# Layer 0's experts: all tokens sorted into 39 blocks of 128 rows, one expert per block, outputs gathered back inside the cross-attention

## The chip, the cores and the metric

The kernel runs on one core of one Trainium2 chip. The metric is the device time of one execution in microseconds (us); three executions of the kernel before give a median of 1479.89 us.

## The reference, cut to what matters

A perceiver of two layers works on `x`, 128 batches of 32 tokens of 128 values, so 4096 tokens. Each layer adds three things to `x`: a cross-attention over a context of 257 rows for each batch, a self-attention, and a feed-forward part made of experts. The change is in the experts of layer 0 and touches the cross-attention of layer 1 that comes next. The experts of layer 0 are:

```python
capacity = ceil(T / E * 1.25)                 # T = 4096 tokens, E = 8 experts: 640
...
top1_idx = argmax(probs, axis=-1)             # the expert that each token wants
keep = position of the token in its expert (by falling probability) < capacity
final_e = where(keep, top1_idx, 0)            # dropped tokens go to expert 0
...
for e in range(E):
    h = relu(tokens @ W1[e] + b1[e])          # 128 -> 512
    y = h @ W2[e] + b2[e]                     # 512 -> 128
    out = out + where((final_e == e)[:, None], y, 0.0)
```

Experts 1 to 7 hold at most 640 tokens each; expert 0 holds its own and all dropped ones, so its size has no bound below 4096. The sum over experts is added to `x`, and the layer norm ahead of the next cross-attention reads the result.

## The kernel before

The 4096 tokens lie as 32 groups of 128 rows (`G = 32`), `X[:, g, :]` on the 128 partitions. All products are in fp32. The kernel is a row of phases, each a block with its own semaphores and a barrier of all engines at its end; inside a phase each engine runs a program written out by hand, and the engines meet only at semaphores. Matmuls run on TensorE (PE), and GpSimd (POOL) issues the DMAs whose rows are picked by a table of indices.

- `attend_layer0` does layer 0's two attentions. It leaves the normed tokens in `H_all`, their transposes in `HT_all`, and the router's logits. On the side its sync queue zeroes `rows_out` in memory.
- `route_layer0` (names that begin with `r_`) finds each expert's cut-off probability by 13 rounds of bisection: VectorE (DVE) counts, PE sums the counts over partitions (L987), DVE narrows. Then it computes for each token of experts 1 to 7 a slot number in a table of 7 x 640 rows. PE fills its gaps with `dense` pieces: expert 0 on every token of the first 20 groups, 512 tokens at a time (L948 up, L957 down).
- `experts_layer0` (`f_`) first turns the slot table round into `token_of`, the token of each slot, by 32 accumulating matmuls (L1193). It computes expert 0 on the other 12 groups (L1174, L1183) and adds expert 0's result to `X` under `MASK`. Then for each expert 1 to 7: five indirect gathers of rows of `rows_h` (L1330), transposes (L1211), the up product (L1221) in halves of 320 columns, ReLU on ScalarE (ACT), the down product (L1233), the bias on DVE (L1407), and five indirect scatters into `rows_out` (L1338). After the experts, `weights` computes 14 pieces of a weight product for the layer 1 self-attention (L1254, L1261). At the end the sync queue (SP) loads `rows_out` back into `HT_all` in 8 pieces (L1163).
- `cross_layer1` (`c_`) goes over 32 groups of 4 batches, four steps to a group. Its prologue loads `last`, the last context row of each batch (L1691), and norms group 0. The loaded expert outputs are added to `X` by eight wide additions, the first in the phase before (L1413), the others in group 0 (L2057).
- `experts_layer1` (also `f_`) works on sorted blocks: for each block of 256 rows a table gives the expert, an engine reads the number into a register, DVE copies that expert's first weights into a small ring `w1b` (L1573), and PE picks the second weights by the register (L1481 transpose, L1490 up, L1500 down).

## Time and profile before

| | |
|---|---|
| runs | 1474.99, 1479.89, 1480.83 us; median 1479.89 |
| profiled execution | 1482.46 us, of which the span of the trace is 1480.7 |
| PE | busy 1315.8 us, 89% of the span |
| PE weight loads | 1008.5 us, 68% |
| DVE | 1041.4 us, 70% |
| ACT | 821.3 us, 55% |
| POOL | 671.8 us, 45% |
| `route_layer0`, first PE work to that of `experts_layer0` | 319.68 to 373.08 us |
| `experts_layer0` to the first PE work of `cross_layer1` | 373.08 to 507.77 us |

Busy shares are means over phases with different limits. PE's busy time is modelled from pipelined matmuls, so the start-to-start distance of its rows tells more than their duration. An fp32 matmul shows as two rows, an fp32 transpose as one.

### The profile page before, as it was taken

Reading aid. Unit: us, or ns where it says so; the run is one execution under the profiler, and the core shown is the slowest. Engines: PE = TensorE matmul, PEld = TensorE weight load, DVE = VectorE, ACT = ScalarE, POOL = GpSimd, SP = SyncE. Lnnn points to the kernel's source line nnn. Section 1 sums busy time; section 2 is a strip of 40 time slices with the busy share of each in tenths; the row PEclk is TensorE's granted clock in tenths of the full one; section 3 lists DMA queues with packets and bytes.
Section 4 is the critical chain, followed back from the end, with each engine's and each line's share of the span. In section 5 each row is a group of like instructions: output and inputs, shape, how many; then the busy total and the mean of one; then the engine's idle time right before and its main releaser. Section 6 shows DMA issues by size and latency. Waiting matters only on the chain. (4 is left out here: it accounts for less than half of the span.)

```text
span 1480.7 us, 40476 instructions
## 1 busy us (share of the span) xinstructions
PE 1315.8 (89%) x14596; PEld 1008.5 (68%) x14596; DVE 1041.4 (70%) x3345; ACT 821.3 (55%) x2488; POOL 671.8 (45%) x1270
## 2 busy tenths in 40 slices
PE   4898998879999699999999999969999999986981
PEld 2676766646677567777777777757878788775960
DVE  2899999947322288888888888846788888884433
ACT  3566666533233278888888888833444444443630
POOL 2455555420457335444454444532224444555773
PEclk9999999989799789999999999989999999997995
DMA  6656744210111322222222222200000000003425
GB/s 192 203 180 200 247 126 152 65 58 1 32 33 39 102 66 81 73 78 80 70 81 73 78 81 70 78 3 1 2 3 14 16 12 16 19 26 83 116 71 176
DMA packets 78484, 114.66 MB, mean 77 GB/s; under 512 B 12480, under 2 KB 55753, under 8 KB 78160
## 3 DMA queue, kind: packets, MB, share of 16 engines
q1 hardware_dynamic: 70352, 97.93, 21.3%
q0 software_dynamic: 6784, 12.06, 2.6%
q8 instruction: 119, 1.95, 0.5%
q10 hardware_dynamic: 1152, 2.10, 0.4%
q14 instruction: 77, 0.63, 0.1%
HBM read 78.95 MB, written 35.00 MB: 77 GB/s over the span
## 5 line engine op out<-in xcount | busy, mean ns | idle before, releaser
L1862 ACT ACTIVATE c_pr<-c_pS,c_nm 128x257 f32<-128x257 f32 x512 | 236.3, 474 | 75.3 <-DVE c_nm L1992 74.4
L1992 DVE TENSOR_REDUCE c_nm<-c_pS 128x1 f32<-128x257 f32 (+1 forms) x384 | 173.5, 507 | 30.8 <-PE c_pS L1731 30.8
L2340 ACT ACTIVATE s_k<-s_pK 128x512 f32<-128x512 f32 x128 | 76.4, 597 | 156.7 <-PE s_pK L2226 156.7
L2226 PEld LDWEIGHTS s_pK<-s_hT,AH 128*128 128x128 f32 x1024 | 126.1, 198 | 21.4 <-ACT s_k L2340 16.7
L2226 PE MATMUL s_pK<-s_hT,AH 128*128 128x128 f32 x1024 | 139.7, 287 | 0.5 <-ACT s_hT L2335 0.5
L1735 PE MATMUL c_pT<-cst,c_pr 128*128 128x128 f32 x1024 | 133.7, 274 | 0.0
L1735 PEld LDWEIGHTS c_pT<-cst,c_pr 128*128 128x128 f32 x1024 | 116.9, 142 | 0.4 <-issue 0.4
L2001 DVE COPY c_prT<-c_pT 128x512 f32<-128x512 f32 x128 | 88.5, 692 | 24.6 <-PE c_pT L1735 24.5
L1862 ACT ACTIVATION_READ_ACCUMULATOR c_pr<-c_pS,c_nm 128x1 f32 x512 | 104.0, 203 | 0.0
L2253 PE MATMUL s_pM<-BH,s_uT 128*128 128x128 f32 x832 | 98.2, 275 | 0.0
L2253 PEld LDWEIGHTS s_pM<-BH,s_uT 128*128 128x128 f32 x832 | 95.5, 192 | 0.0
L1731 PE MATMUL c_pS<-c_ks,c_qq 32*128 32x257 f32 x1024 | 94.2, 432 | 0.0
L1564 POOL DMA_INDIRECT rows_out<-f_yb,f_token_of x78 | 77.6, 995 | 35.4 <-issue 18.9
L1722 PE MATMUL c_pM<-wsq,c_ctxT 128*128 128x128 f32 x512 | 92.6, 304 | 0.6 <-ACT c_ks L1856 0.6
L1722 PEld LDWEIGHTS c_pM<-wsq,c_ctxT 128*128 128x128 f32 x512 | 67.9, 193 | 27.4 <-issue 18.8
L1742 PE MATMUL c_pO<-c_prT,c_vs 128*32 128x128 f32 x2048 | 82.7, 279 | 1.5 <-ACT c_prT L1877 1.2
L1717 PE MATMUL c_pM<-c_ctxT,wsq 128*128 128x257 f32 x256 | 82.3, 404 | 1.7 <-DVE c_vs L1996 1.7
L1877 ACT ACTIVATE c_prT<-c_pT 128x512 f32<-128x512 f32 x128 | 77.8, 608 | 1.3 <-PE c_pT L1735 1.3
L1742 PEld LDWEIGHTS c_pO<-c_prT,c_vs 128*32 128x32 f32 x2048 | 48.0, 109 | 44.4 <-issue 20.3
L1936 POOL TENSOR_TENSOR c_half<-c_om 128x256 f32<-128x256 f32 x32 | 23.4, 732 | 119.9 <-DVE c_om L2015 119.9
L2418 POOL DMA_INDIRECT rows_in<-HH,slots x64 | 64.5, 1008 | 21.4 <-issue 21.4
L1731 PEld LDWEIGHTS c_pS<-c_ks,c_qq 32*128 32x128 f32 x1024 | 41.9, 185 | 43.5 <-issue 43.5
(414 smaller groups left out, 3317.2 us busy)
## 6 DMA issues: line engine op xcount, KB each, us to landing
rows_in<-c_blank SPq DMA_DIRECT2D x32, 520.0 KB, 3.2
a_ctxT<-in_ctxT SPq DMA_DIRECT2D x32, 514.0 KB, 3.9
c_ctxT<-in_ctxT SPq DMA_DIRECT2D x128, 128.5 KB, 2.2
a_ctxN<-in_ctxR SPq DMA_DIRECT2D x32, 512.0 KB, 4.4
hb<-rows_in SPq DMA_DIRECT2D x39, 130.0 KB
f_w<-in_f_w SPq DMA_DIRECT2D x16, 256.0 KB, 3.6
a_ctxL<-in_ctxL SPq DMA_DIRECT2D x128, 16.0 KB, 3.8
f_w<-in_f_w SPq DMA_DIRECT2D x16, 128.0 KB, 3.7
```

The costliest lines, as they stand in the source:

```text
L1564: pool.indirect_dma_start(rows_out, bass.IndirectOffsetOnAxis(ap=token_of[:, i, j:j + 1], axis=0), yb[:, i % RB, j, :], None, bounds_check ...
L1717: pe.matmul(pM[:, 0:S], w("wk1"), ctxT[:, b, :], start=True, stop=True).then_inc(k_done.sem, 1)
L1722: mm = pe.matmul(pM[:, c * D:(c + 1) * D], ctxT[:, b, c * P:(c + 1) * P], w("wv1"), start=True, stop=True)
L1731: pe.matmul(pS[:, c, 0:S], qq[r, b % 2, :, :], ks[r, b % 2, :], start=True, stop=True).then_inc(s_done.sem, 1)
L1735: mm = pe.transpose(pT[:, c, j, :], pr[:, b % 2, j, c * P:(c + 1) * P], k("ident"))
L1742: mm = pe.matmul(pO[j * T:(j + 1) * T, b, :, :], vs[:, b, c, j * T:(j + 1) * T], prT[:, b % 2, c, j, :], start=(c == 0), stop=(c == SC - 1 ...
L1862: act.activation(pr[:, b % 2, c, :], pS[:, c, 0:S], ACT.Exp, bias=nm[:, c:c + 1], accum_out=den[:, b % 2, c:c + 1]).then_inc(e_ready.sem, 1)
L1877: act.activation(prT[:, b % 2, 0, :, :], pT[:, 0, :, :], ACT.Copy).then_inc(pT0_ready.sem, 1)
L1992: dve.tensor_reduce(nm[:, c:end], pS[:, c:end, 0:S], AX.X, ALU.max, negate=True).then_inc(max_ready.sem, 1)
L2001: dve.tensor_copy(prT[:, b % 2, 1, :, :], pT[:, 1, :, :]).then_inc(pT1_ready.sem, 1)
L2226: mm = pe.matmul(pK[:, c % 2, i, :], AH[:, c * HK + i, :], hT[:, p, :], start=True, stop=True)
L2253: mm = pe.matmul(pM[:, 0, :], uT[:, h, :, :], BH[:, h, :], start=False, stop=(h == H - 1))
```

## The change

Expert 0 is sorted like the others. The counts of all eight experts are rounded up to whole blocks of 128 rows; (4096 + 8 x 127) / 128 gives room for 39 blocks, and all 39 are always computed. Routing also makes a table with the expert of each block (`expert0_i`) and the first bias of each block (`b1c0`), and the 14 pieces of the weight product stand in its rounds, where the dense pieces stood. The experts phase is the loop of `experts_layer1` on blocks of 128 rows. Outputs are stored in block order with plain DMAs (`rows_y`), and `cross_layer1` gathers each group's rows back with an indirect DMA on POOL and adds them on DVE, group by group. `rows_out`, its zeroing, the scatters, `y0` and the masked additions are gone.

```diff
+BLOCKS0 = (B * T + E * (P - 1)) // P      # 39
+RH0, RY, BACKS = 12, 8, 4                 # rings: gathered rows, outputs, rows gathered back
@@ attend_layer0, sync queue
-                for g in range(G // E * e, G // E * (e + 1)):
-                    sp.dma_start(env["rows_out"][g * P:(g + 1) * P, :], zero[:, :]).then_inc(env["rows_zeroed"], 16)
@@ route_layer0, tensor
-            pe.wait_ge(env["ew_loaded"][0], 32 * E)
-            dense(8)
+            for c in range(NF):
+                mm = pe.transpose(pW[0:E, 3, c, :], vec[:, VB1_0 + c:VB1_0 + E * NF:NF], k("ident"))
+            mm.then_inc(b1T_done.sem, 1)
+            weight_product(0)
+            weight_product(1)
...
             for n in range(ROUNDS):
                 pe.wait_ge(count_ready.sem, n + 1)
                 pe.matmul(pC[:, 0:4], peers[:, :], count[:, :], start=True, stop=True).then_inc(total_ready.sem, 1)
-                dense(3 if n % 3 == 0 else 2)
+                if n + 2 < PIECES:
+                    weight_product(n + 2)
...
-            pe.matmul(pC[:, 9:10], earlier[:, :], scan2[:, N - 1:N], start=True, stop=True).then_inc(base_total.sem, 1)
+            pe.matmul(pC[:, 9:10], earlier[:, :], scan2[:, N - 1:N], start=True, stop=True)
+            pe.matmul(pQ[:, 0:1], peers[:, :], scan2[:, N - 1:N], start=True, stop=True)
+            pe.matmul(pQ[:, 2:3], k("before"), k("ones")[:, 0:1], start=True, stop=True).then_inc(base_total.sem, 1)
+            pe.wait_ge(blocks_ready.sem, 1)
+            pe.matmul(pQ[:, 1:2], ahead[:, :], blocks[:, :], start=True, stop=True).then_inc(start_total.sem, 1)
...
+            pe.matmul(pE, k("ones"), past[:, :], start=True, stop=True).then_inc(expert_done.sem, 1)
+            for c in range(NF):
+                mm = pe.matmul(pD[:, c, :], b1T[:, c, :], mine[:, :], start=True, stop=True)
@@ route_layer0, vector
-            then(dve.tensor_scalar(base[:, :], pC[:, 9:10], slot0[:, :], None, ALU.add))
+            then(dve.tensor_scalar(blocks_i[:, :], pQ[:, 0:1], float(P - 1), None, ALU.add))
+            then(dve.tensor_single_scalar(blocks_i[:, :], blocks_i[:, :], 7, ALU.logical_shift_right))
+            dve.tensor_copy(own[:, :], pQ[:, 2:3])
+            dve.tensor_copy(blocks[:, :], blocks_i[:, :]).then_inc(blocks_ready.sem, 1)
+            then(dve.tensor_scalar(before0[:, :], pC[:, 9:10], -1.0, None, ALU.add))
+            then(dve.scalar_tensor_tensor(base[:, :], pQ[:, 1:2], float(P), before0[:, :], ALU.mult, ALU.add))
...
+            dve.tensor_copy(expert0_i[:, :], pE)
+            then(dve.tensor_copy(expert[:, :], pE))
+            dve.tensor_scalar(mine[:, :], expert[0:E, :], own[0:E, :], None, ALU.is_equal).then_inc(mine_ready.sem, 1)
@@ experts_layer0, tensor
+            def turn(j):
+                pe.wait_ge(h_loaded[j % RH0], 16 * (j // RH0 + 1))
+                pe.matmul(pT[:, j % 2, 0:P], h[:, j % RH0, :], k("ident"), start=True, stop=True).then_inc(hT_done, 1)
+            def up(j):
+                pe.wait_ge(hT_ready, j + 1)
+                pe.wait_ge(w1b_ready, j + 1)
+                for c in range(NF):
+                    mm = pe.matmul(chunk(j, c), w1b[:, j % RW, c * P:(c + 1) * P], hT[:, j % 2, :], start=True, stop=True)
+            def down(j):
+                e = pe.value_load(expert_i[0:1, j:j + 1], min_val=0, max_val=E - 1)
+                for c in range(NF):
+                    mm = pe.matmul(pY[:, j % 2, 0:D], hid[:, j % RHID, c, :], w2[:, bass.ds(e, 1), c, :].rearrange("p e d -> p (e d)"), ...)
+            token_numbers()
+            turn(0); turn(1); up(0)
+            for j in range(BLOCKS0): turn(j + 2); up(j + 1); down(j)
@@ experts_layer0, vector: w1b copy two blocks ahead, the last quarter of the ReLU, the bias
+            for j in range(BLOCKS0): weights(j + 2); hidden(j + 1); outputs(j)
@@ cross_layer1
+            def gather_back(g):
+                if g >= BACKS:
+                    pool.wait_ge(back_added.sem, g - BACKS + 1)
+                pool.indirect_dma_start(back[:, g % BACKS, :], None, env["rows_y"], bass.IndirectOffsetOnAxis(ap=env["slot_of"][:, g:g + 1], axis=0), ...)
...
+                    if b == 2 and g > 0 and g + BACKS - 1 < G:
+                        gather_back(g + BACKS - 1)
...
+            for r in range(RY):
+                pool.wait_ge(env["y_stored"][r], 16 * ((BLOCKS0 - r + RY - 1) // RY))
+            for g in range(BACKS):
+                gather_back(g)
             n4.gpsimd(pool, 0)
...
+            def add_back(g):
+                dve.wait_ge(env["back_gathered"][g % BACKS], 16 * (g // BACKS + 1))
+                dve.tensor_tensor(x_of(g), back[:, g % BACKS, :], x_of(g), ALU.add).then_inc(back_added.sem, 1)
```

(The lines of the two loops over `BLOCKS0` and of `turn`, `up` and `down` are joined and shortened here.)

How the instructions move is seen best in the order in which each engine's stand. On PE, at the start of routing and through its first rounds, before (`r_pR<-r_count` is the sum of a round, `r_pH` and `r_pY` are dense pieces):

```order
L948 MATMUL r_pH<-HT_all,f_w 128x512 x8
L983 MATMUL r_pR<-cst,r_pm 128x128 x2
L987 MATMUL r_pR<-r_count,r_peers 128x4
L957 MATMUL r_pY<-f_w,r_hid 128x128 x12
L987 MATMUL r_pR<-r_count,r_peers 128x4
L957 MATMUL r_pY<-f_w,r_hid 128x128 x4
L948 MATMUL r_pH<-HT_all,f_w 128x512
```

and now (`r_pW` are the bias transposes and the pieces of the weight product):

```order
L968 MATMUL r_pW<-cst,vec 8x128 x4
L957 MATMUL r_pW<-cst,wqkv 128x128 x8
L976 MATMUL r_pR<-cst,r_pm 128x128 x2
L980 MATMUL r_pR<-r_count,r_peers 128x4
L957 MATMUL r_pW<-cst,wqkv 128x128 x4
L980 MATMUL r_pR<-r_count,r_peers 128x4
```

Eight wide products ahead of the transposes of `r_pm` have become twelve transposes, and each round carries four small instructions where it carried eight to twelve products.

On PE at the start of the experts phase, before:

```order
L1174 MATMUL f_pH<-HT_all,f_w 128x512 x4
L1193 MATMUL f_pT<-f_in_block,H_all 128x35 x32
L1174 MATMUL f_pH<-HT_all,f_w 128x512 x4
L1183 MATMUL f_pY<-f_w,f_hid 128x128 x16
L1174 MATMUL f_pH<-HT_all,f_w 128x512 x4
L1183 MATMUL f_pY<-f_w,f_hid 128x128 x32
L1211 MATMUL f_pT<-cst,f_h 128x128 x5
```

and now, where `TENSOR_LOAD` and `ISA` are the register work that picks the expert:

```order
L1173 MATMUL f_pT<-f_in_block,H_all 128x39 x32
L1180 MATMUL f_pT<-cst,f_h 128x128 x2
L1189 MATMUL f_pH<-f_hT,f_w1b 128x128 x4
L1180 MATMUL f_pT<-cst,f_h 128x128
L1189 MATMUL f_pH<-f_hT,f_w1b 128x128 x4
L1193 TENSOR_LOAD expert_i
L1193 ISA x2
L1199 ISA
L1199 MATMUL f_pY<-f_w,f_hid 128x128
```

The token numbers stand first, and nothing stands between them and the first transposes of gathered rows; after that a block is one transpose, four up and four down products.

On POOL in a group of the cross-attention, around the third and fourth of its four steps, now (before, the same rows stood without the `DMA` row):

```order
L1829 TENSOR_TENSOR c_rq<-c_rinv,cst 128x512
L1850 TENSOR_TENSOR c_tot<-c_osum,c_left 128x128
L1810 DMA c_back<-rows_y,slot_of 128x128
L1818 TENSOR_TENSOR c_qq<-c_q,cst 128x128
L1826 COPY c_pl<-c_pr 128x4
L1855 TENSOR_TENSOR c_xb<-X,bo 128x128
```

The gather stands in front of `c_qq`, which PE needs for the next step's scores.

## Rows read from the trace of the kernel before

**Rows 1.** Windows: busy us (instructions) of each engine, granted clock, DMA share, GB/s

```profile
380.00:391.00 11.00, 11.00 (x63) 10.89 (x63) 2.52 (x4) 0.47 (x1) 1.06 (x1) 0.61 0.00 0
600.00:800.00 200.00, 198.94 (x2430) 144.39 (x2433) 165.22 (x435) 164.79 (x591) 97.08 (x226) 1.00 0.25 77
1353.00:1355.00 2.00, 2.00 (x7) 1.62 (x6) 0.29 (x1) 1.11 (x3) 0.00 (x0) 0.50 0.46 117
1355.00:1357.00 2.00, 2.00 (x15) 1.92 (x14) 0.55 (x3) 1.22 (x3) 0.00 (x0) 0.92 0.42 104
```

**Rows 2.** Timeline of PE in routing: start us, us, idle before and its releaser

```profile
336.83 0.39 PE L987 MATMUL r_pR<-r_count,r_peers 128*128 128x4 f32 x2 [0.18 <-DVE r_hit L1069]
339.25 0.39 PE L987 MATMUL r_pR<-r_count,r_peers 128*128 128x4 f32 x2 [0.21 <-DVE r_hit L1069]
342.22 0.28 PE L987 MATMUL r_pR<-r_count,r_peers 128*128 128x4 f32 x2
```

**Rows 3.** Timeline of DVE in routing

```profile
329.50 0.42 DVE L1065 COPY r_pmT<-r_pR 128x256 f32<-128x256 f32 x1 [3.54 <-PE r_pR L983]
369.44 0.22 DVE L1087 TENSOR_SCALAR r_base<-r_pR,r_slot 128x1 f32<-128x1 f32 x1 [0.47 <-PE r_pR L997]
```

**Rows 4.** Timelines of PE and POOL at the start of the experts phase

```profile
379.59 11.02 PE L1193 MATMUL f_pT<-f_in_block,H_all 128*128 128x35 f32 x64
...
373.62 1.56 POOL L1324 TENSOR_TENSOR f_in_block<-f_in_block,token 128x280 f32<-128x280 f32 x1 [50.38 <-DVE f_in_block L1359]
375.57 1.57 POOL L1324 TENSOR_TENSOR f_in_block<-f_in_block,token 128x280 f32<-128x280 f32 x1 [0.39 <-DVE f_in_block L1359]
...
392.06 1.29 POOL L1330 DMA_INDIRECT f_h<-rows_h,f_token_of  x1 [11.00 <-DVE f_token_of L1372]
393.66 1.00 POOL L1330 DMA_INDIRECT f_h<-rows_h,f_token_of  x1 [0.31 <-issue]
```

**Rows 5.** Timelines of PE and DVE between experts and cross-attention

```profile
488.90 2.78 PE L1254 MATMUL f_pH<-cst,wqkv 128*128 128x128 f32 x24
507.77 0.48 PE L1826 MATMUL c_pS<-cst,c_last 128*128 128x128 f32 x1 [10.04 <-DMA c_last<-in_ctxL]
510.28 0.48 PE L1707 MATMUL c_pS<-cst,c_n_h 128*128 128x128 f32 x1 [0.44 <-DVE c_vl L2067]
...
501.15 0.69 DVE L1413 TENSOR_TENSOR X<-HT_all,X 128x512 f32<-128x512 f32 x1 [11.10 <-DMA HT_all<-rows_out]
```

**Rows 6.** The chain that ended last: a scatter's issue and its landing

```profile
1456.36 0.97 POOL rows_out L1564
1457.63 2.10 DMA rows_out<-f_yb,f_token_of
```

**Rows 7.** Timeline of PE in layer 1's block loop: its start, and one block later on

```profile
1349.54 1.22 PE L1481 MATMUL f_pT<-cst,hb 128*128 128x128 f32 x4 [6.13 <-DMA hb<-rows_in]
...
1400.16 1.03 PE L1490 MATMUL f_pH<-f_hT,f_w1b 128*128 128x256 f32 x4
1401.03 1.05 PE L1500 MATMUL f_pY<-f_w,f_hid 128*128 x8
1401.92 0.38 PE L1481 MATMUL f_pT<-cst,hb 128*128 128x128 f32 x2
1402.14 1.03 PE L1490 MATMUL f_pH<-f_hT,f_w1b 128*128 128x256 f32 x4
```

**Rows 8.** Timelines of DVE and ACT: the copy of weights, two 128x128 operations

```profile
1400.90 0.29 DVE L1573 COPY f_w1b<-f_w 128x256 f32 x1 [0.25 <-issue]
1402.87 0.56 DVE L1573 COPY f_w1b<-f_w 128x256 f32 x1 [0.25 <-issue]
...
509.88 0.35 DVE L2067 TENSOR_SCALAR c_vl<-c_pS,vec 128x128 f32<-128x128 f32 x1 [0.89 <-PE c_pS L1829]
...
510.80 0.28 ACT L1867 ACTIVATE c_hT<-c_pS 128x128 f32<-128x128 f32 x1 [12.27 <-PE c_pS L1707]
```

**Rows 9.** Timelines of DVE, POOL and PE in one cross-attention group

```profile
700.97 1.36 DVE L1992 TENSOR_REDUCE c_nm<-c_pS 128x1 f32<-128x257 f32 x3 [0.70 <-PE c_pS L1731]
...
701.15 0.40 POOL L1912 TENSOR_TENSOR c_qq<-c_q,cst 128x128 f32<-128x128 f32 x1 [0.83 <-ACT c_q L1873]
...
703.73 0.71 PE L1731 MATMUL c_pS<-c_ks,c_qq 32*128 32x257 f32 x8
```

More of the change, by code:

```diff
@@ L926, in _ @@
             act.activation(e8[:, :, :], d[:, :, :], ACT.Exp).then_inc(e_ready.sem, 1)
[L927 to L940 removed]
+            act.wait_ge(b1T_done.sem, 1)
@@ L962, in _ @@
-            given, LAST = [0], (2 * DENSE - 1) * NF
-            def dense(pieces):
-                for i in range(given[0], given[0] + pieces):
-                    n, j = divmod(i - NF, 2 * NF)
-                    if i < NF:
-                        up(0, i)
-                    elif i >= LAST:
-                        down(DENSE - 1, i - LAST)
-                    elif j < NF:
-                        up(n + 1, j)
-                    else:
-                        down(n, j - NF)
-                given[0] += pieces
@@ L1060, in _ @@
             dve.wait_ge(tables_ready.sem, 4)
-            then(dve.tensor_reduce(slot0[:, :], slot_e[:, :], AX.X, ALU.add))
-            then(dve.tensor_scalar(slot0[:, :], slot0[:, :], -1.0, None, ALU.add))
             then(dve.memset(ones[:, :], 1.0))
@@ L1273, in _ @@
+            pe.wait_ge(env["ew_loaded"][0], 32 * E)
+            token_numbers()
+            pe.wait_ge(number_ready, 1)
+            turn(0)
+            turn(1)
+            up(0)
+            for j in range(BLOCKS0):
+                if j + 2 < BLOCKS0:
+                    turn(j + 2)
+                if j + 1 < BLOCKS0:
+                    up(j + 1)
+                down(j)
         @block.scalar
         def _(act):
-            def dense():
-                for r in range(LATE):
-                    if r > 1:
-                        act.wait_ge(down_done, r - 1)
-                    for c in range(NF):
-                        m = r * NF + c
-                        act.wait_ge(up_done, m + 1)
-                        act.activation(hid[:, r % 2, c, 0:N], pH[:, m % 4, :], ACT.Relu, bias=vec[:, VB1_0 + c:VB1_0 + c + 1]
-                                       ).then_inc(up_ready, 1)
@@ L1317, in _, with turned @@
-            all_phases(dense, sorted_, weights)
+            def turned(j):
+                act.wait_ge(hT_done, j + 1)
+                if j > 1:
+                    act.wait_ge(up_done, j - 1)
+                act.activation(hT[:, j % 2, :], pT[:, j % 2, 0:P], ACT.Copy).then_inc(hT_ready, 1)
+            turned(0)
+            turned(1)
+            for j in range(BLOCKS0):
+                act.wait_ge(up_done, j + 1)
+                if j >= RHID:
+                    act.wait_ge(down_done, j - RHID + 1)
+                for c in range(ACT_F):
+                    act.activation(hid[:, j % RHID, c, :], chunk(j, c), ACT.Relu, bias=b1c[:, c, j:j + 1]).then_inc(up_kept, 1)
+                if j + 2 < BLOCKS0:
+                    turned(j + 2)
@@ L1411, in _ @@
-            all_phases(dense, sorted_, weights)
-            dve.wait_ge(env["back_loaded"][0], 16)
-            dve.tensor_tensor(X[:, 0:TG, :], back[:, 0:TG, :], X[:, 0:TG, :], ALU.add).then_inc(added, 1)
+            for j in range(2):
+                weights(j)
+            hidden(0)
+            for j in range(BLOCKS0):
+                if j + 2 < BLOCKS0:
+                    weights(j + 2)
+                if j + 1 < BLOCKS0:
+                    hidden(j + 1)
+                outputs(j)
```

422 lines of the change are left out of this document (151 added, 271 removed).

## The prediction

> **What bounds the kernel now.** I read the windows first, stage by stage. In the long cross-attention PE is busy 198.94 of 200 us at full clock and DVE 165.22 [rows 1]: a PE stage with a little room on the other engines. Then the timeline of routing. The sum of a round on PE comes 2.42 us after the last one when two dense pieces lie between (336.83 to 339.25, then PE idles 0.21 for DVE) and 2.97 us when three do (to 342.22, no idle) [rows 2]. So DVE sets most rounds, and PE the 5 of 13 that carry three pieces. The experts phase starts on a PE that is 11.00 of 11 us busy, but at a granted clock of 0.61 [rows 1], half speed for most of it. Its sorted loop is PE's from end to end, and its products end at 488.90, where the weight product starts. After that all wait for DMAs: DVE 11.10 us for the rows loaded back, PE 10.04 us for `c_last`, and the first normed group is transposed at 510.28 [rows 5]. From there on the two kernels run nearly alike. So the sum asks one thing: when does this transpose start now?
>
> **Routing.** Before, its first PE work is at 319.68 and that of the experts phase at 373.08 (both in the table).
> The start: DVE waits 3.54 us because eight wide dense products stand ahead of the transposes of `r_pm` [rows 3]. Now twelve transposes stand there. Such a transpose takes 2.78 / 24 = 0.12 us at full clock [rows 5], 0.24 at half; 2.9 us in all, over before DVE is ready. Two small `slot0` operations go too, 0.5. Gain 4.0.
> The rounds: five fall from 2.97 to 2.42, gain 2.7. Against it PE has less to do, and if that leaves it at half clock, each trip to PE (DVE idles 0.47 for one at full clock [rows 3]) grows, say by 0.15, 1.9 over 13 rounds. Gain 0.8, with bounds -1.2 and 2.7.
> The tail: between `scan2` and `slots` DVE did one small operation after one trip. Now five stand on the path, 0.25 start to start (0.22 each [rows 3]), and a second trip of 0.5 to 0.7: +1.8. After `lane_of` come three more small ones, four small products, an ACT copy of 0.28 [rows 8] and the waits between: +2.0. Half clock may add 0.5, which I count.
> Sum: -4.0 - 0.8 + 4.3 = -0.5; bounds -3 and +2.5. The experts phase starts at 372.6.
>
> **Up to the first block.** The token numbers started at 379.59, behind 6.5 us of dense work, though POOL's first chunk was ready at 375.18 [rows 4], 2.1 us into the phase; now they start there. They took 11.02 us at mostly half clock; with no dense work ahead of them I take 12. At full clock it would be some 7.3 (64 rows at 0.114), but the four chunks come 1.95 us apart [rows 4], so not below 8. They end at +14.1. From their end (390.61) to the first gather's issue (392.06) is 1.45, the second gather starts 1.6 later [rows 4], and one lands 3.4 us after its issue starts (1456.36 to 1459.73 [rows 6]). The first up product stands behind the second transpose, +0.4: 14.1 + 1.45 + 1.6 + 3.4 + 0.4 = 20.95, that is 393.6. Before, 20 us of dense work covered this wait; the cover is gone, and the wait counts in full.
>
> **The 39 blocks.** The nearest rows are layer 1's loop, with the same order, rings and register loads. Its four 128-column products take 0.89 start to start, 0.222 each, and the next block starts 1.98 after the last with no idle [rows 7]: the register load is hidden. A block here is nine products of that width, 9 x 0.222 = 2.0. The other engines need less: DVE 0.25 of load gap, the copy of 128x512 (between the 0.29 of 128x256 and twice it, say 0.43), the last quarter of the ReLU and the bias at 0.35 each, 1.4; ACT four of 0.28 and two waits, 1.4 [rows 8]; POOL 1.3 for a gather [rows 4]; SP one plain store. So 39 x 2.0 = 78.0. The clock: PE idles ahead of the loop. Layer 1's loop starts at 1349.54 after a wait of 6.13 [rows 7], is still at 0.50 until 1355 and at 0.92 after it [rows 1]: 5.6 us at half speed, 2.8 lost. The last product ends at 393.6 + 80.8 = 474.4, where before it was 488.90.
>
> **From the last product to the norm.** The weight product's tail goes, and with it the eight loads of 256 KB ahead of `c_last`. New is a chain: the bias 0.4; a plain store, issued and landed, 2.8 (bounds 2.1 and 3.4, by the landing in [rows 6]); four gathers of 1.3 on POOL, 5.2, because the norm's root stands behind all four on POOL; the root with its steps 0.85; the scaling 0.35 [rows 8]; gaps 0.6. That is 10.2. The load of `c_last` and its small steps (2.5 from 507.77 to 510.28 [rows 5]) run beside it. The transpose starts at 484.6: 25.7 before 510.28.
>
> **The cross-attention.** Each group adds one gather on POOL and one 128x128 addition on DVE (about 0.3 with its wait). The addition falls where DVE waits 0.70 for scores. The gather takes 1.0 to 1.8; `c_qq` behind it started at 701.15 after 0.83 of idle, and the scores that read it start at 703.73 [rows 9]. Even 1.8 us from 700.32 lets it end by 702.6. The transfer itself has three groups' time. Both cost nothing so; without that cover 1.3 or 0.3 in each of some 29 groups. Seven wide additions leave group 0, and 32 zero stores the first stage, where a sync queue carried them beside full engines: nothing for either.
>
> **The sum** is 1482.46 - 25.7 = 1456.8 against the profiled execution, which stands 2.6 above the median; against the median it is 1454.2. I say 1455.
>
> **Rivals.** (a) DVE becomes the bound of the block loop. The 128x256 copy took 0.29 once and 0.56 another time while POOL issued DMAs [rows 8]. If the 128x512 copy takes twice 0.56, DVE needs 0.25 + 1.1 + 0.35 + 0.35 and two waits, 2.3 a block: 39 x 0.3 = +12, so 1467. For it: POOL issues a gather a block all through. Against: half of layer 1's copies came through unhurt though POOL never rested there.
> The Trainium skill speaks for (a) (SBUF — State Buffer, Who interferes with whom): a VectorE copy in a two-port mode and a GpSimd instruction exclude each other for the whole instruction. The doubled copy agrees. By that rule each copy could wait out a gather's issue of 1.0 us, and the loop would stand at 2.3 to 2.4 us a block.
> (b) The addition reaches the path of the cross-attention: 31 x 0.3 = +9, so 1464. For it: DVE is busy 165 of 200 us. Against: the gap of 0.70 is just where the addition falls.
> (c) Slower than before: the gather holds `c_qq` back until PE waits in every group. It decides from 0.9 us a group, since 29 x 0.9 is the gain; the full 1.3 gives +38, so 1493. For it: POOL works in order and `c_qq` is next. Against: 1.1 us of slack by the rows above.
> (d) Two of these together, or a loop at 2.5 us a block: about 1475, no change that can be told.
> (e) The open costs all fall well (token numbers 4 shorter, full clock early 2.8, landings short 2.6): 1446.
>
> **How the numbers follow.** The forecast's own case, with (e), holds 1446 to 1462: 0.66. (a) 0.11, (b) 0.12, (d) 0.05, (c) 0.06. The range 1444 to 1469 takes in e, a and b. A measurement of this kernel can tell about 0.5%, 7.4 us, from no change. Faster 0.89, the same 0.05, slower 0.06.
>
> **What would show it.** Blocks 2.0 us apart on PE without idle, DVE busy under 1.8 in each; the first up product near 394 and the last down near 474; PE idle for some 5 us after the token numbers and 10 after the last block; routing rounds of 2.4 to 2.6; groups of the cross-attention as far apart as before, 14.2 us. A block distance over 2.2 with DVE full is (a), groups 0.3 longer (b), groups over 15 with PE waiting for `c_qq` (c). The prediction is wrong above all if the loop cannot keep 2.0 us a block.

## The result and the profile after

The changed kernel takes 1461.01 us (median of 4 runs, 1459.87 to 1464.81) against 1480.33 for the kernel before on the same chip: a ratio of 0.9882, 95% interval 0.9853 to 0.9911, or 19.3 us less. Measured a second time on another occasion it took 1458.59 (6 runs, 1455.22 to 1463.85) against 1476.76, ratio 0.9871 (0.9848 to 0.9893). The forecast was 1455 in 1444 to 1469: the sign and the range held, the gain was some 6 us smaller than the forecast's 25.7. The profiled execution took 1461.19, its span is 1459.4, 21.3 less than before.

Windows of the changed kernel, the columns as in [rows 1]: most of routing, its tail, the token numbers, the first blocks, the other blocks, the start of the cross-attention, and its steady part.

```profile
330.00:362.00 32.00, 27.12 (x105) 22.93 (x105) 22.38 (x121) 7.53 (x12) 0.00 (x0) 0.50 0.00 0
362.00:377.00 15.00, 7.66 (x28) 6.42 (x28) 6.89 (x28) 0.22 (x1) 0.00 (x0) 0.50 0.00 1
380.00:395.00 15.00, 13.84 (x64) 13.73 (x64) 7.45 (x9) 0.00 (x0) 5.05 (x4) 0.50 0.05 21
401.00:406.00 5.00, 5.00 (x29) 5.00 (x28) 1.24 (x3) 2.12 (x8) 3.78 (x5) 0.58 0.18 49
406.00:481.00 75.00, 74.83 (x671) 74.65 (x670) 36.20 (x111) 42.74 (x147) 33.79 (x32) 1.00 0.21 57
481.00:491.00 10.00, 2.20 (x9) 1.15 (x7) 2.86 (x11) 0.00 (x0) 5.78 (x8) 0.64 0.50 152
600.00:800.00 200.00, 198.93 (x2432) 144.27 (x2430) 167.81 (x449) 164.96 (x592) 113.08 (x241) 1.00 0.27 81
```

The third column from the right is what to look at: PE is granted half of its clock (0.50, 1.2 GHz) from routing until the loop of blocks is under way, some 80 us. Once the loop runs, it is PE's without a gap (74.83 of 75 us), and DVE has half of its time left (36.20). In the cross-attention DVE has 2.6 us and POOL 16.0 us more work than in [rows 1], and PE as much as before.

The timeline of PE from routing to the cross-attention, piece by piece:

```profile
329.62 0.59 PE L980 MATMUL r_pR<-r_count,r_peers 128*128 128x4 f32 x2 [2.30 <-DVE r_hit L1070]
332.25 0.59 PE L980 MATMUL r_pR<-r_count,r_peers 128*128 128x4 f32 x2 [1.09 <-DVE r_hit L1070]
...
380.32 13.84 PE L1173 MATMUL f_pT<-f_in_block,H_all 128*128 128x39 f32 x64 [3.57 <-POOL f_in_block L1240]
398.89 0.77 PE L1180 MATMUL f_pT<-cst,f_h 128*128 128x128 f32 x2 [4.73 <-DMA f_h<-rows_h,f_token_of]
400.66 1.70 PE L1189 MATMUL f_pH<-f_hT,f_w1b 128*128 128x128 f32 x7
...
415.79 0.39 PE L1180 MATMUL f_pT<-cst,f_h 128*128 128x128 f32 x2
416.90 1.06 PE L1199 MATMUL f_pY<-f_w,f_hid 128*128 x8
417.80 0.39 PE L1180 MATMUL f_pT<-cst,f_h 128*128 128x128 f32 x2
...
480.21 1.15 PE L1199 MATMUL f_pY<-f_w,f_hid 128*128 x8 [0.17 <-ACT f_hid L1231]
484.89 0.48 PE L1725 MATMUL c_pS<-cst,c_last 128*128 128x128 f32 x1 [3.52 <-DMA c_last<-in_ctxL]
490.66 0.45 PE L1606 MATMUL c_pS<-cst,c_n_h 128*128 128x128 f32 x1 [3.70 <-DVE c_n_h L228]
...
599.57 0.39 PE L1660 MATMUL c_pM<-wsq,c_on 128*128 128x128 f32 x2
613.80 0.39 PE L1660 MATMUL c_pM<-wsq,c_on 128*128 128x128 f32 x2
```

The reader sees the rounds 2.63 apart, with PE waiting 1.09 for DVE in each; the token numbers, which keep PE busy for 13.84 us; a wait of 4.73 for the gathered rows; blocks 2.01 apart (415.79 to 417.80); and the normed group transposed at 490.66, 19.6 before the 510.28 of [rows 5]. Groups of the cross-attention are 14.23 apart, as they were. What the other engines do at these places:

```profile
384.67 1.62 POOL L1240 TENSOR_TENSOR f_in_block<-f_in_block,token 128x312 f32<-128x312 f32 x1 [0.42 <-DVE f_in_block L1258]
395.62 1.52 POOL L1251 DMA_INDIRECT f_h<-rows_h,f_token_of  x1 [9.32 <-DVE f_token_of L1271]
417.05 1.00 POOL L1251 DMA_INDIRECT f_h<-rows_h,f_token_of  x1 [0.30 <-issue]
488.25 1.00 POOL L1810 DMA_INDIRECT c_back<-rows_y,slot_of  x1 [0.30 <-issue]
...
377.98 0.48 DVE L1258 TENSOR_TENSOR f_in_block<-lanes,block_of 128x312 f32<-128x312 f32 x1 [3.22 <-PEq L91]
394.20 0.20 DVE L1269 TENSOR_SCALAR f_number<-f_pT 128x39 f32<-128x39 f32 x1 [6.86 <-PE f_pT L1173]
417.24 0.43 DVE L1279 COPY f_w1b<-f_w 128x512 f32 x1 [0.85 <-PE f_pH L1189]
487.77 0.29 DVE L1968 TENSOR_TENSOR X<-c_back,X 128x128 f32<-128x128 f32 x1 [0.42 <-DMA c_back<-rows_y,slot_of]
490.17 0.35 DVE L228 TENSOR_SCALAR c_n_h<-X,c_n_mv,c_n_rstd 128x128 f32<-128x128 f32 x1 [1.45 <-POOL c_n_rstd L224]
```

POOL is done with its last chunk at 386.29, and DVE waits 6.86 and POOL 9.32 us for PE alone. Before, the token numbers and dense work on expert 0 shared this stretch of PE.

It pays to cut both traces at the same events and to compare the pieces, because the piece ahead of routing varies from one execution to the next by up to 4 us, as shown below. All numbers are differences of row starts; the last down product counts by its end (before, by the start of the weight product at 488.90). The column "forecast" has the shares from the prediction's own steps.

| us | before | forecast | after | mix | mix_fp16 |
|---|---|---|---|---|---|
| first PE work of routing at | 319.68 | 319.68 | 321.76 | 320.67 | 321.16 |
| to the sum of round 1 | 11.82 | 7.8 | 7.86 | 7.85 | 7.86 |
| 12 rounds more | 30.77 | 30.0 | 31.53 | 29.69 | 30.17 |
| to DVE's first work of the experts phase | 10.81 | 15.1 | 16.83 | 15.42 | 15.00 |
| to the token numbers | 6.51 | 2.1 | 2.34 | 2.33 | 2.32 |
| to the first gather's issue | 12.47 | 13.45 | 15.30 | 15.30 | 8.28 |
| to the first up product | none | 5.4 | 5.04 | 4.97 | 5.03 |
| 39 blocks, to the end of the last down product | none | 80.8 | 80.70 | 80.41 | 80.26 |
| to the transpose of the normed group | 21.38 | 10.2 | 9.30 | 8.76 | 8.73 |
| routing's start to that transpose | 190.60 | 164.9 | 168.90 | 164.73 | 157.65 |

(Before had no such loop: from the first gather's issue, 392.06, to the transpose it is 118.22, of which the last 21.38, from 488.90, stand in the row that answers to the chain.) Two more profiled executions of the same pieces, of the changed kernel run again and of the kernel called no_back below, give 168.93 and 168.91 for the last line: in these three, what follows routing's start is the same to 0.03 us.

The column "before" is less firm, and this bears on all that follows. The run called b_noweights below has the code of the kernel before up to the last down product. Its pieces are 11.94, 32.38, 10.81, 5.76 and 10.04 from routing's start to the first gather's issue, 70.93 where the table has 72.38, and 188.82 to the transpose where it has 190.60. The 1.6 us more in the rounds are all in the first one (4.60 instead of 3.00), at a granted clock of 0.71; the rounds behind it agree to 0.01. The 2.4 us less ahead of the gather are the token numbers, 8.59 instead of 11.02. The window of its first round:

```profile
335.00:340.00 5.00, 2.89 (x14) 2.88 (x14) 3.81 (x19) 0.52 (x1) 0.00 (x0) 0.71 0.00 0
```

So the pieces gained 21.7 us against the one trace and 19.9 against the other; the medians say 19.3 and 18.2.

### The profile page after: what moved, and what is told of

It reads as the page before. It is cut to its first block and busy times, and to the rows that moved or that the text cites. A ratio compares the mean times of both kernels' runs of the same rounds, so it can differ in the third digit from the quotient of the medians.

```text
span 1459.4 us, 41219 instructions
## 1 busy us (share of the span) xinstructions
PE 1287.9 (88%) x14536; PEld 1008.6 (69%) x14536; DVE 1058.8 (73%) x3416; ACT 815.4 (56%) x2567; POOL 678.3 (46%) x1270
```

## Experiments

### The clock in routing: warm_route and warm_both

warm_route puts products of 512 columns, whose results nobody reads (fillers), into PE's gaps in routing: four at the start, one in each round, four in the tail.

```diff
+            def filler(times):
+                for i in range(times):
+                    pe.matmul(pF[:, :], k("ident"), env["HT_all"][:, 0:TG, :].rearrange("p g t -> p (g t)"), start=True, stop=True)
...
+            filler(4)
             pe.wait_ge(env["factors_loaded"], 32)
             weight_product(0)
...
                 if n + 2 < PIECES:
                     weight_product(n + 2)
+                filler(1)
```

> The changed kernel with idle-time filler on PE in routing only: a 512-column product (transposed tokens against the identity, into an unused bank) four times ahead of the first weight pieces, once in each of the 13 rounds and four times in the tail. The output is the reference's. Theory A: PE stays at 1.2 GHz from 321 us on because its work there is narrow or rare, and that is what made routing 2.8 us longer than before and not 0.5 shorter. Then the granted clock of the rounds rises to near 1.0, the rounds come 2.42 us apart and not 2.63 (2.7 us less), each trip of the tail is 0.2 shorter, and the time falls by 3 to 5 us against the changed kernel (1461), after up to 3 us lost at the start of routing. Theory B: the rounds are DVE's and the filler only stands in the way of PE's sums: rounds at 2.9 or more, 3 to 6 us slower, whatever the clock.

It took 1458.54 us (5 runs, 1456.45 to 1458.81; before on the same chip 1479.20; ratio 0.9846, 0.9823 to 0.9868). The window of routing, and a row of its tail:

```profile
330.00:362.00 32.00, 27.67 (x132) 16.65 (x132) 24.54 (x131) 7.53 (x12) 0.00 (x0) 1.00 0.00 1
...
374.60 2.08 PE L970 MATMUL r_pF<-HT_all,cst 128*128 128x512 f32 x2
```

The granted clock is 1.00 where it was 0.50, and the 12 rounds take 29.04 instead of 31.53, which is 2.42 each: at full clock a round is DVE's and the trips', and each trip at half clock costs 0.21. But the fillers at the start delay the first sum by 1.4, and the last one (374.60) stands ahead of the phase's barrier, so that the tail takes 18.09 against 16.83. From routing's start to the transpose it is 169.13 against 168.90. The mechanism is shown; as a version it gains nothing in the trace, and the lower median does not prove a gain.

warm_both has the same in the experts phase too: two fillers ahead of the token numbers, one ahead of each later chunk, five behind them.

```diff
+                filler(2)
                 for g in range(G):
+                    if g % GC == 0 and g > 0:
+                        filler(1)
...
             token_numbers()
+            filler(5)
```

> As the run with filler in routing, and also filler at the start of the experts phase: two wide products ahead of the token numbers, one ahead of each later chunk, five between the token numbers and the first transpose of gathered rows. The output is the reference's. Theory A: token numbers from 13.8 us down to 9 or 10, since they are held by the four chunks that come 2.04 us apart, and the first two blocks of the loop at 2.0 us and not near 4: 4 to 7 us less than with filler in routing alone. Theory B: the token numbers are narrow products, and the clock stays or falls to half in them whatever surrounds them; the filler at half clock costs 0.85 us more for each piece on the path, so no gain or up to 4 us slower than with filler in routing alone.

Its time is 1459.04, but its six runs spread from 1453.30 to 1465.76, and the profiled one is the longest. In it PE was busy without a gap, and stayed at half clock all the same:

```profile
380.00:400.00 20.00, 20.00 (x69) 15.35 (x69) 7.79 (x8) 0.00 (x0) 5.77 (x4) 0.50 0.06 23
```

The pieces to the transpose sum to 172.85. So the filler only lengthened the phase in that execution. The other runs have no trace, but each has its mean granted clock on record: 0.947 for the profiled one, and 0.957, 0.960 and 0.957 for those of 1456.78, 1453.30 and 1454.46 us, where the runs of warm_route have 0.948 to 0.954. As the clock has two levels, 0.010 more of 1455 us is an estimated 29 us fewer at the lower one. So in three of six runs the clock was up for longer than in the trace, and two of them fell where theory A put them. That the longer stretch lies in the experts phase is not shown: the runs of the kernel before differ by as much without any filler (0.951 to 0.962 in the last series).

### The start of the cross-attention: prologue

```diff
-            pool.memset(blank[:, :, 0:D], 0.0).then_inc(blank_ready.sem, 1)
-            pool.memset(blank[:, :, D:DQ], NO_TOKEN).then_inc(blank_ready.sem, 1)
...
-            for g in range(BACKS):
-                gather_back(g)
+            gather_back(0)
+            gather_back(1)
+            pool.memset(blank[:, :, 0:D], 0.0).then_inc(blank_ready.sem, 1)
+            pool.memset(blank[:, :, D:DQ], NO_TOKEN).then_inc(blank_ready.sem, 1)
             n4.gpsimd(pool, 0)
             n4.gpsimd(pool, 1)
+            for g in range(2, BACKS):
+                gather_back(g)
```

DVE also takes the addition and the statistics of group 0 ahead of `vl`.

> The changed kernel with the start of the cross-attention reordered and nothing else: POOL gathers groups 0 and 1 before it clears the blank tile (1.06 us), computes both roots of the norm before it gathers groups 2 and 3, and DVE adds and takes the statistics of group 0 before the last context row's bias. The output is the reference's. My theory of that stretch is that store, gather, addition, root and scaling form one chain: then the first normed group is transposed 1 to 1.6 us earlier against the last block's end (9.3 us now), and the time falls by as much. The rival is that the load of the last context row and its small steps bound it (first PE work 3.5 us after the last block for that DMA): then less than 0.4 us changes.

1457.91 us (5 runs, 1457.43 to 1459.85), ratio 0.9851 (0.9829 to 0.9873). POOL's timeline:

```profile
482.74 1.00 POOL L1808 DMA_INDIRECT c_back<-rows_y,slot_of  x1 [29.96 <-DMA rows_y<-f_y]
487.33 0.57 POOL L224 TENSOR_TENSOR c_n_rstd<-c_n_ve,cst 128x1 f32<-128x1 f32 x1
```

From the last down product to the transpose it takes 8.62 instead of 9.30, from routing's start 167.89 instead of 168.90. The first gather is issued 2.92 behind the last product and was at 2.97, so the clearing of the blank tile ahead of it had held nothing up: the wait is for the store. The norm's root (`c_n_rstd`) stood behind all four gathers, as the forecast had said. With two of them (2.6 us) behind it, what it waits for next is the addition on DVE, which waits 1.39 for the first landing, so that only 0.7 to 1.0 of the 2.6 is gained.

### The order of the first transposes: turn_late

```diff
             turn(0)
-            turn(1)
             up(0)
+            turn(1)
```

> The changed kernel with one exchange on PE: the first block's up product stands ahead of the second block's transpose. The output is the reference's. If the wait for the second gather is on the path, as the prediction counted it (1.6 us between the first two gathers, 0.4 for the transpose), the first up product starts 1.0 to 1.4 us earlier. But what follows needs the second and third blocks at half clock, where a block takes near 4 us against 1.3 of a gather, so the whole may gain the same 1 us. The rival: the ScalarE copy between the second transpose and the second up product is then uncovered, and up to 0.9 us of it is given back, total within 0.4 us.

1458.68 us (5 runs, 1457.67 to 1459.99), ratio 0.9851 (0.9829 to 0.9873). The first up product comes 4.38 after the first gather's issue instead of 5.04, but the blocks take 81.49 instead of 80.70, and the sum to the transpose is 168.98 against 168.90: nothing. In the changed kernel PE is busy without a gap from the first up product on (5.00 of 5 us in the window 401 to 406), at a clock of 0.58. It has the same work to do in either order at that clock, and the fourth block's transpose comes 10.24 behind the first gather's issue where it came 10.12.

### Is the gather back hidden? no_back

after_again is the changed kernel once more, as the baseline.

> The changed kernel, nothing altered, as the baseline of the three others on this chip. Both theories expect 1461 us, within 0.2% of its first measurement.

no_back leaves out the gather and the addition for groups 4 to 31.

```diff
-                    if b == 2 and g > 0 and g + BACKS - 1 < G:
+                    if b == 2 and g > 0 and g + BACKS - 1 < BACKS:
                         gather_back(g + BACKS - 1)
-                    if b == 2 and g + 2 < G:
+                    if b == 2 and g + 2 < BACKS:
                         add_back(g + 2)
```

> Leaves out the gather and the addition of layer 0's expert outputs for groups 4 to 31, so most of that term is missing from x. If the gather and the addition are hidden in every group of the cross-attention, as the distance of 14.23 us in both traces says, the time stays within 0.5 us of the changed kernel, 1460.5 to 1461.5. If they cost what rivals (b) or (c) ask, 0.3 or 1.3 us in each of 28 groups comes back: 1453 or 1425.

Both took 1458.59 us (6 runs, and 4 runs of 1457.21 to 1462.80). The steady part of no_back:

```profile
600.00:800.00 200.00, 198.94 (x2431) 144.32 (x2430) 165.12 (x437) 164.91 (x590) 96.16 (x224) 1.00 0.25 77
```

DVE and POOL have what they had before the change, PE the same 198.9. From the transpose to the end of the span it is 967.3 against 967.7 in after_again. The gathers and additions cost nothing, as forecast, and rivals (b) and (c) are excluded.

### What a block costs: blocks36 and copies3

```diff
-BLOCKS0 = (B * T + E * (P - 1)) // P
+BLOCKS0 = 36
```

> 36 blocks instead of 39, nothing else (with these inputs the blocks that go may hold tokens; those are left out). PE bounds the loop at 2.01 us a block: three blocks less give 6.0, so 1455. If DVE or the gathers' issue on POOL set the distance the result is the same per block, but the first blocks at the lower clock stay; if the loop's length is hidden behind another wait after it, the gain is under 3.

1450.42 us (4 runs, 1450.22 to 1450.95), 8.2 under the changed kernel. The loop takes 74.70 instead of 80.70: exactly three blocks of 2.0. All other pieces from routing's start to the transpose together are 0.13 shorter (162.77 against 168.90). Where the 2 us beyond the expected 6 come from is open. The two profiled executions (1450.95 and 1462.72) differ by 3.6 us more ahead of routing, which starts at 320.70 and 324.29, and by 2.0 more behind the transpose, which takes 965.7 and 967.7; the edit touches neither place.

```diff
+                for i in range(2):
+                    dve.tensor_copy(w1x[:, i, j % RW, :], w1[:, bass.ds(experts[j], 1), :].rearrange("p e f -> p (e f)"))
                 dve.tensor_copy(w1b[:, j % RW, :], w1[:, bass.ds(experts[j], 1), :].rearrange("p e f -> p (e f)")).then_inc(w1b_ready, 1)
```

> The changed kernel with two more copies of the first weights per block, into tiles that nobody reads. A copy took DVE 0.43 us in the trace of the changed kernel, up to 0.54 beside POOL's issues, and DVE is busy 36 of 75 us in the loop, 0.94 a block of 2.01. If that is all (the forecast), a block needs 1.8 to 2.0 of DVE and the loop stays within 0.1 a block, 0 to 4 us more in all. If a copy can wait for POOL's issue of 1.0 us (rival (a)), DVE passes 2.01 clearly and the loop grows by 0.5 or more a block, 20 us.

1461.85 us (4 runs, 1460.90 to 1463.15). The loop takes 83.66 instead of 80.70, 0.08 a block. Its window, and the groups of DVE in 408 to 470 (count, busy us and mean ns):

```profile
406.00:481.00 75.00, 74.73 (x647) 73.74 (x645) 58.21 (x180) 41.86 (x144) 35.09 (x32) 1.00 0.21 56
...
L1281 DVE COPY f_w1x<-f_w 128x512 f32 x60 | 23.5, 434 | 13.4 <-issue 13.4
L1282 DVE COPY f_w1b<-f_w 128x512 f32 x29 | 12.2, 422 | 0.0
```

Three times the copies leave each at 0.42 to 0.43 us, with POOL issuing a gather a block, and DVE, busy 58.21 of 75 us, still holds PE up by only 3 us in 39 blocks. This excludes rival (a). The copy of the changed kernel at 417.24 lies within the gather's issue from 417.05 to 418.05 and takes 0.43; twelve of the 39 start within such an issue, and over all 39 the median is 0.427 and the longest 0.542. So no copy here waited for the rest of an issue of 1.0 us. The rule that the forecast took from the Trainium skill for rival (a) (SBUF — State Buffer, Who interferes with whom), that the two exclude each other for the whole instruction, would have had these twelve wait; the rows do not bear it out for a gather's issue as POOL's records show it, and the measurement decides.

### Was the weight product hidden? b_noweights

The kernel before, without the 14 pieces of the weight product at the end of its experts phase.

```diff
-                for m in range(PIECES):
-                    weight_product(m)
```

> The kernel before without the 14 pieces of the weight product at the end of its experts phase; two ACT copies of other data fill the places of their results, so the later self-attention computes something else. The forecast says that this product stood on nothing: from the last down product the normed group waits for scatters, loads back and c_last. Then the time is that of the kernel before, within 1 us, 1476 to 1477 against 1476.8 in the last series. If it did hold up the phase, the time falls by up to the 12 us that the pieces take on PE.

1481.33 us (10 runs, 1476.41 to 1484.17) against 1475.38, ratio 1.0021 (1.0001 to 1.0041): no gain. PE now waits nearly twice the 10.04 us of [rows 5]:

```profile
511.50 0.47 PE L1827 MATMUL c_pS<-cst,c_last 128*128 128x128 f32 x1 [19.24 <-DMA c_last<-in_ctxL]
504.41 0.69 DVE L1414 TENSOR_TENSOR X<-HT_all,X 128x512 f32<-128x512 f32 x1 [11.17 <-DMA HT_all<-rows_out]
```

The last down product ends at 492.26, so `c_last` is transposed 19.24 behind it; in the kernel before it was 18.87 behind the start of the weight product. The product was fully hidden behind the scatters and the loads back; the change gained by taking these away, not by moving the product. In this execution routing starts at 325.18, 5.5 us later than in the trace of the kernel before, and the pieces from there to the transpose are 1.8 shorter. Why the median is 6 us higher was not settled.

### A version that beats both: mix, mix_narrow, mix_fp16

mix has the prologue above and fillers only where they held nothing up: one ahead of the first piece, one behind the transposes of `r_pm`, one a round, two in the tail.

```diff
+            filler(1)
             pe.wait_ge(env["factors_loaded"], 32)
...
             mm.then_inc(pmT_done.sem, 1)
+            filler(1)
...
                     weight_product(n + 2)
+                filler(1)
...
+            filler(1)
             pe.wait_ge(keep_ready.sem, 1)
...
+            filler(1)
             pe.wait_ge(rank_ready.sem, 1)
```

> A version meant to be faster than both kernels. It has the reordered prologue of the cross-attention, and wide filler products in routing, but only where the trace of the first filler kernel showed that they held nothing up: one ahead of the first pieces of the weight product, one behind the transposes of r_pm, one per round, and one ahead of each of the first two waits of the tail. The fillers' results are never read. Theory A (the lost time is PE at the lower clock in routing): rounds at 2.42 instead of 2.63 give 2.5, the tail 1.0 to 2.5, the prologue 1.0, together 4.5 to 6 below the changed kernel, 1455.5 to 1457. Theory B (rounds and tail are set by DVE and by trips between engines, and the first filler kernel gained by chance): the prologue alone, 1460.

1454.74 us (5 runs, 1453.25 to 1455.73), ratio 0.9840 (0.9820 to 0.9860), 3.9 under the changed kernel on the same chip. By the table the rounds give 1.8, the tail 1.4, the prologue 0.5 to 0.9, in sum 4.2: a little under what was expected, for theory A. The clock is not up from the first round: it is 0.81 from 330 to 335 us and 1.00 from 335 on.

mix_narrow splits each filler into four products of 128 columns.

```diff
-                    pe.matmul(pF[:, :], k("ident"), env["HT_all"][:, 0:TG, :].rearrange("p g t -> p (g t)"), start=True, stop=True)
+                    for q in range(TG):
+                        pe.matmul(pF[:, q * P:(q + 1) * P], k("ident"), env["HT_all"][:, q, :], start=True, stop=True)
```

> As mix, but each filler product of 512 columns is four of 128 columns: as many columns, four times the instructions and weight loads. If what lifted the granted clock is that PE is busy at all, it is lifted here too and rounds stay at 2.42 us. If narrow products do not lift it, as the token numbers (39 columns, PE busy without a gap at 0.50) suggest, the granted clock stays at 0.50 in routing and each round is longer than 2.63, since the filler then takes its time at half speed: 1458 or more.

1455.28 us (4 runs, 1453.69 to 1455.76), ratio 0.9847 (0.9816 to 0.9878). Its window of routing:

```profile
330.00:362.00 32.00, 28.84 (x210) 26.55 (x209) 24.06 (x126) 7.52 (x12) 0.00 (x0) 0.95 0.00 1
```

My expectation was wrong here: products of 128 columns lift the clock as well as those of 512 (rounds 29.71 against 29.69). The 39 columns of the token numbers are narrower still, and this run says nothing about them.

mix_fp16 is mix with the two masks of the token numbers, `in_lane` and `in_block`, in 16-bit floats. The integers from -2048 to 2047 are exact in them, so the offset of the numbers changes; an empty slot now names token 2048, whose row is computed there and read by nobody.

```diff
-            pool.tensor_scalar(token[:, :], token[:, :], -float(2 * TOKENS), None, ALU.add)
+            pool.tensor_scalar(token[:, :], token[:, :], -float(TOKENS // 2), None, ALU.add)
...
-        in_lane = env["H_all"]
+        in_lane = sb("in_lane", [P, G, P], F16)
...
-                dve.tensor_scalar(number[:, :], pN, float(2 * TOKENS), None, ALU.add).then_inc(number_ready, 1)
+                dve.tensor_scalar(number[:, :], pN, float(TOKENS // 2), None, ALU.add).then_inc(number_ready, 1)
```

> The version called mix, and in it the two masks of the token numbers in 16-bit floats (a token number less 2048 is exact in them), which halves the rows on PE. In the changed kernel the token numbers took PE 13.84 us from 380.32 while POOL had its last chunk ready at 386.29 and DVE was free at 387.4. Theory A (PE at the lower clock is what the phase waits for): they end just behind POOL's last chunk, the first gather is issued 6 to 7 us earlier after the phase's start than in the changed kernel (17.64 there), and the time is 6 below mix, some 1449 against 1455. Theory B (DVE and POOL set it, so PE's share is hidden): less than 2 us earlier.

1448.55 us (5 runs, 1446.05 to 1450.27) against 1475.38, ratio 0.9805 (0.9778 to 0.9832). It is the fastest version: by the medians 6.7 under mix_narrow of the same series, and 6.2 under mix and 10 under the changed kernel of an earlier series, on another chip; in the pieces it is 7.1 under mix (157.65 against 164.73) and 11.25 under the changed kernel (168.90). Timelines of PE, DVE and POOL:

```profile
376.51 0.43 PE L1184 MATMUL f_pT<-f_in_block,f_in_lane 128*128 128x39 f16 x8 [3.57 <-POOL f_in_block L1251]
382.62 0.43 PE L1184 MATMUL f_pT<-f_in_block,f_in_lane 128*128 128x39 f16 x8 [1.61 <-POOL f_in_block L1251]
388.05 0.77 PE L1191 MATMUL f_pT<-cst,f_h 128*128 128x128 f32 x2 [5.00 <-DMA f_h<-rows_h,f_token_of]
...
382.19 1.34 DVE L1310 MEMSET f_h<- 128x1536 f32 x1 [0.27 <-issue]
384.79 1.52 POOL L1262 DMA_INDIRECT f_h<-rows_h,f_token_of  x1 [2.31 <-DVE f_token_of L1282]
```

Eight groups take 0.43 us, where they took 13.84 / 4 = 3.46, and now PE waits for POOL. The first gather is issued 8.28 behind the token numbers' start instead of 15.30, 7.0 earlier: theory A. DVE and POOL take as long for the masks as before (a chunk's `in_block` 0.98 and 1.62 us), so the gain is PE's alone. A clearing of `h` on DVE (1.34) is next in line.

## Why the prediction was right, and where its size was off

**What held.** The sum asked when the first normed group is transposed, and this carried. The loop is PE's at 2.01 us a block (forecast 2.0, confirmed by three blocks taken away), 80.70 with its start at half clock (80.8). The start of routing gained 3.96 (4.0), and the copy of `r_pm` transposed no longer waits. The expert products' old end, bound by scatters, loads back and `c_last`, was the thing gained (b_noweights), and the chain in its place took 9.30 (10.2). From the end of the last bias to the first gather's issue, the store took 2.53 where 2.8 was allowed, the four gathers 4.95 for 5.2, and the gap at the end 0.14 for 0.6. The cross-attention costs nothing.

**The rounds and the tail of routing** were the largest error: forecast -0.5 in all, measured +2.8 (56.22 against 53.40). The rounds' part of it leans on the trace of the kernel before, whose PE rows are here:

```profile
331.50 0.38 PE L987 MATMUL r_pR<-r_count,r_peers 128*128 128x4 f32 x2 [2.10 <-DVE r_hit L1069]
334.50 0.28 PE L987 MATMUL r_pR<-r_count,r_peers 128*128 128x4 f32 x2
...
362.27 0.39 PE L987 MATMUL r_pR<-r_count,r_peers 128*128 128x4 f32 x2
```

The rounds were put at -0.8 and came to +0.76. The step "if that leaves it at half clock, each trip to PE ... grows, say by 0.15" was in the sum with its right sign; it is 0.21 (2.63 against 2.42, warm_route), 2.5 in 12 rounds. And the gain of the long rounds was counted in full as 2.7, whereas in the kernel before a long round was followed by a short one (334.50, then 336.83: 2.33): 30.77 less 12 x 2.42 leaves only 1.7. Against the 32.38 of b_noweights the rounds came to -0.85, by chance what was forecast, because the first round of the kernel before was slow there. The cost of 2.5 stands in either case. The tail was put at +4.3 and came to +6.0 (10.81 in both traces of the kernel before): 0.8 of it ahead of the mask, 2.3 for the second trip and its small operations (forecast 1.8), 2.6 from `lane_of` to the phase's start (2.0), and 0.3 between them. All at half clock, for which 0.5 was allowed. mix gets 1.4 of it back.

**Up to the first block** was put at 20.95 from the phase's start and took 22.68. The term that was too small is "they took 11.02 us at mostly half clock; with no dense work ahead of them I take 12". They took 13.84, which is all of them at half clock: 64 rows at 0.216. In the kernel before, the token numbers began at full clock and fell to half on the way, with PE busy throughout:

```profile
381.00:382.00 1.00, 1.00 (x12) 1.00 (x11) 1.00 (x1) 0.00 (x0) 0.06 (x1) 1.00 0.00 0
383.00:384.00 1.00, 1.00 (x6) 1.00 (x6) 0.00 (x0) 0.00 (x0) 0.00 (x0) 0.50 0.00 0
```

The full clock at their start came with the dense work ahead of them, and that went with the change. In b_noweights it lasted longer, to 391 of 386.07 to 394.66, hence the 8.59 there. The landing was 0.4 better. That this term stands on the path in full is shown by mix_fp16, which gets 7.0 us by it.

Against the profiled execution that the forecast started from, these errors add up: 3.3 + 1.7 - 0.1 - 0.9 = 4.0, just the difference between -25.7 and the -21.7 measured from routing's start to the transpose.

**The first stage** was put at nothing. In the two traces routing starts at 319.68 and 321.76, and nothing here shows that the change made any of these 2.1 us. A part of 0.6 arises within the first six groups of the first attention (the first operation of the seventh group's top-8 search starts at 71.06 and 71.68 us). Counted from the first group it is 47.31 in the trace of the kernel before and 47.78 to 48.09 in those of the changed kernel and its variants, but 48.16 in b_noweights, which has the code of the kernel before. The rest comes later. These are windows of the changed kernel, of blocks36 and of no_back, which have the same code there:

```profile
292.00:296.00 4.00, 4.00 (x56) 3.12 (x56) 2.07 (x6) 0.66 (x2) 0.00 (x0) 0.57 0.01 4
304.00:308.00 4.00, 2.88 (x73) 1.90 (x72) 1.90 (x6) 2.11 (x5) 2.47 (x4) 1.00 0.00 0
...
292.00:296.00 4.00, 3.60 (x63) 2.83 (x63) 2.85 (x9) 0.94 (x5) 0.00 (x0) 1.00 0.02 4
304.00:308.00 4.00, 3.26 (x103) 2.42 (x102) 2.25 (x6) 1.45 (x4) 2.30 (x4) 1.00 0.00 0
...
292.00:296.00 4.00, 4.00 (x58) 3.23 (x57) 1.79 (x6) 0.66 (x2) 0.00 (x0) 0.57 0.02 4
304.00:308.00 4.00, 3.63 (x41) 2.64 (x39) 1.46 (x4) 0.97 (x3) 2.35 (x4) 0.50 0.00 0
```

Where the pipeline of the first attention runs out, PE has gaps, and in some executions its clock drops for 2 to 4 us, once or twice. Routing then starts at 320.70 (blocks36, no drop), 321.76 (one) or 324.82 (no_back, two). The kernel before had none up to 312 us in its profiled execution, and b_noweights had them (routing from 325.18). Behind the transpose, the changed kernel's trace took 968.7 against 970.4 before, but b_noweights took 967.7, and blocks36 965.7: this is spread of the same kind. The spread goes with the clock: of the fifteen runs of the kernel before in the last series, the fastest (1473.73) has a mean granted clock of 0.962, the slowest (1484.04) one of 0.951. The medians' gains of 19.3 and 18.2 are near the 19.9 of the pieces against the trace of b_noweights and 2 to 3.5 us below the 21.7 against the trace that the forecast started from. So a part of the forecast's excess of 6 us may be the draw of that one execution; how large a part was not settled.

**What stays open.** No single rule of how busy PE is tells here which clock it gets. In routing PE at half clock was busy 27.12 of 32 us by the records, and at full clock 27.67 (warm_route). In the token numbers it was busy without a gap at 0.50, and in the kernel before the clock fell within them. The block loop, products of 128 columns from end to end, had 1.00, and mix_narrow shows that 128 columns are enough to lift it. The products of 39 columns, and those of the weight product with 64 rows in depth, were not tried by themselves.

## What to carry to other kernels

Work that is taken off an engine may have been what kept its clock up: when dense products leave a stretch of small, dependent ones, price everything that stays at half speed, trips included, and look whether a cheap filler that ends before the next wait brings it back. When a covering piece of work goes, the formerly hidden step gets its own line in the sum, at the clock that it will then have; and here the best repair was a smaller step (16-bit masks, 7 us) rather than a higher clock. To compare two traces, cut them at common events: from routing's start to the transpose the changed kernel repeated to 0.03 us in three traces where its runs spread by 8. But take two traces of each kernel: the kernel before differed by 1.8 in the same pieces.

## Not expected of the hardware

A PE that is busy without a gap for 14 us can stay at 1.2 GHz (13.84 us at 0.50 in the token numbers; 20.00 of 20 us in warm_both, though with products of 512 columns between), and one that is at full clock can lose it while busy (1.00 at 381 us, 0.50 at 383, in the token numbers of the kernel before, products of 35 columns), while one product of 512 columns or four of 128 in each round of 2.4 us lifted it to 0.95 or 1.00. A product of 128x39 in fp32 took 0.43 us at half clock (two rows of 0.216), one in 16-bit floats 0.43 / 8 = 0.05. A 128x512 copy on DVE within a gather's issue on POOL took its usual 0.43.
